# Attention with the last quarter of each head mixed by float32 matmuls, and its low halves dropped

## The reference

```python
def _L1_xattn_ref(query, key_value, Wq, bq, Wk, bk, Wv, bv, Wo, bo):
    Q = query @ Wq.T + bq          # (4, 512, 512)
    K = key_value @ Wk.T + bk      # (4, 1024, 512)
    V = key_value @ Wv.T + bv
    ...                            # into 16 heads of 32
    scores = jnp.einsum('bhsd,bhtd->bhst', Q, K) * scale
    attn = jax.nn.softmax(scores, axis=-1)
    ctx = jnp.einsum('bhst,bhtd->bhsd', attn, V)
    return ctx.transpose(0, 2, 1, 3).reshape(B, S, D_MODEL) @ Wo.T + bo
```

## Time and profile before

| | us |
|---|---|
| median of 3 runs | 1690.8 |
| lowest, highest | 1686.87, 1693.01 |
| the profiled execution, its own time | 1685.53 |
| its span, first to last instruction | 1683.8 |
| attention phase, first `maximum` to last store (window 729 to 1225) | about 496 |
| steady part, heads 0 to 56 | 405.94 |
| last seven heads | 44.93 |

### The profile page before, as it was taken

How to read it: one execution, slowest core, us unless ns; L and a number is a source line. 1 busy time by engine, 2 the same in 40 slices (tenths; PEclk the granted TensorE clock), 3 DMA queues, 4 the chain that set the end, 5 groups by cost and what they waited for, 6 DMA issues and landing times. The chain is left out here.

```text
span 1683.8 us, 27138 instructions
## 1 busy us (share of the span) xinstructions
PE 1411.4 (84%) x10011; PEld 811.6 (48%) x10087; DVE 1215.8 (72%) x1489; ACT 946.8 (56%) x1440; POOL 528.6 (31%) x403
## 2 busy tenths in 40 slices
PE   4999996999851975878998899998777699999996
PEld 3555543555430543314554555555323566666663
DVE  4888855678762878578999899999487676655551
ACT  5887833445440865406666676766622776655551
POOL 0122200000053006207887788887920000000000
PEclk7999998999965987869999999999988799999998
DMA  6788760000046439300434242533372786666640
GB/s 225 232 274 308 240 210 26 1 1 1 1 197 254 138 108 222 113 26 20 96 69 92 62 102 62 102 77 110 73 226 105 236 279 215 216 205 221 226 146 27
DMA packets 162676, 233.25 MB, mean 139 GB/s; under 512 B 46396, under 2 KB 80191, under 8 KB 161416
## 3 DMA queue, kind: packets, MB, share of 16 engines
q1 hardware_dynamic: 157064, 206.60, 40.8%
q0 software_dynamic: 5504, 25.20, 4.1%
HBM read 169.62 MB, written 55.65 MB: 134 GB/s over the span
## 5 line engine op out<-in xcount | busy, mean ns | idle before, releaser
L1707 POOL TENSOR_TENSOR t_low<-t_e 128x1024 bf16<-128x1024 f32 x192 | 375.2, 1979 | 79.2 <-DVE t_low L1796 48.7
L1750 ACT ACTIVATE t_e<-t_psE 128x512 f32<-128x512 f32 x512 | 278.0, 595 | 150.7 <-PE t_psE L1883 149.9
L1788 DVE TENSOR_REDUCE t_nmax<-t_psM 128x1 f32<-128x1024 f32 x256 | 303.4, 1215 | 27.4 <-PE t_psM L1861 26.4
L1897 PE MATMUL t_psO<-t_e,vst 128*33 128x512 bf16 x1024 | 221.4, 396 | 7.4 <-POOL t_low L1707 7.4
L1861 PE MATMUL t_psM<-kst,qst 96*64 96x512 bf16 x1024 | 176.8, 412 | 48.8 <-DVE t_nmax L1788 42.4
L2365 PE MATMUL e_psG<-late_flat,e_w1p 128*128 (+1 forms) x1536 | 171.1, 274 | 15.0 <-DVE e_hT L2309 10.3
L1883 PE MATMUL t_psE<-qst,kst 99*64 99x512 bf16 x1024 | 168.3, 387 | 1.2
L2365 PEld LDWEIGHTS e_psG<-late_flat,e_w1p 128*128 128x128 bf16 x1536 | 150.5, 98 | 35.9 <-issue 8.4
L2380 PE MATMUL e_psO<-e_w2p,e_hT 128*128 128x512 bf16 x752 | 164.9, 379 | 0.8
L1897 PE MATMUL t_psO<-t_low,vst 128*33 128x512 bf16 x512 | 155.8, 386 | 0.0
L1796 DVE TENSOR_TENSOR t_low<-t_e 128x1024 bf16<-128x1024 f32 x64 | 118.9, 1857 | 34.4 <-ACT t_e L1750 34.4
(11 more groups left out here) (262 smaller groups left out, 2300.8 us busy)
## 6 DMA issues: line engine op xcount, KB each, us to landing
piece<-in_L_ffn_w SPq DMA_DIRECT2D x32, 1024.0 KB, 13.8
xres<-in_L_ffn_w SPq DMA_DIRECT2D x32, 1024.0 KB, 14.8
wT<-ternary POOLq DMA_DIRECT2D x8, 1536.0 KB, 20.7
kst<-keys SPq DMA_DIRECT2D x96, 128.0 KB, 3.5
c_rows<-in_ctx SPq DMA_DIRECT2D x8, 1024.0 KB, 9.7
xres<-in_L_ffn_wg SPq DMA_DIRECT2D x8, 1024.0 KB, 7.0
xres<-in_L_ffn_wu SPq DMA_DIRECT2D x8, 1024.0 KB, 6.1
xres<-in_L_ffn_wd SPq DMA_DIRECT2D x8, 1024.0 KB, 6.3
```

The costliest lines, as they stand in the source:

```text
L1707: nc.gpsimd.tensor_tensor(low[:, slot(h, u), :, :], e32[:, slot(h, u), :, :], upper(h, u), ALU.subtract).then_inc(lo_pool, 1)
L1750: nc.scalar.activation(e32[:, slot(h, u), i, :], psE[:, i, :], ACT.Exp, scale=SC).then_inc(expd, 1)
L1788: nc.vector.tensor_reduce(nmax[:, h // G % 2, h % G, u:u + 1], banks_of(place_of_max(b, m)).rearrange("p a t -> p (a t)"), AX_X, ALU.max, ...
L1897: return nc.tensor.matmul(psO[side * SIDE:side * SIDE + VW, h % 2, :], values(i, r), part[:, i, :], start=first, stop=last)
```

## The change

- Quarter 3 (`FULL`) is mixed in float32: two matmuls, one for each block of 128 keys, of the float32 tile `t_e` with a new float32 values tile `t_v` (`v32`). Block 0 goes to side 0 and block 1 to side 1. No low half is made for it.
- `v32` is high plus low of `vst` (`join_values`): four joins on POOL for batch 0 before its first `max_parts`, then one join on VectorE for each group of four heads, three heads after the group's new values are asked for (`next_values`). A memset puts the ones in.
- Low halves of quarters 0 to 2 stay on POOL, and POOL no longer waits for VectorE's (`lo_dve`). In the last seven heads quarter 0 is made on VectorE.
- `t_low` shrinks from eight to six quarters. The second half of the sums lies in the keys tile instead of a tile of its own, so their load moves from head 2 to head 6 of the last batch, the sum and reciprocal on VectorE from head 5 to head 8, and the reciprocals' store from head 6 to head 9. The second spread goes into `v32`.

```diff
--- before.py
+++ after.py
...
     RING = 8
-    LO_ON_POOL = (0, 1, 2)
+    FULL = (3,)
     SIDE = P // 2
...
         e32 = sb("t_e32", [P, RING, 2, S], F32)
-        low = sb("t_low", [P, RING, 2, S], BF16)
+        low = sb("t_low", [P, RING - 2 * len(FULL), 2, S], BF16)
+        v32 = sb("t_v32", [P, G, TC, VW * G], F32)
         nmax = sb("t_nmax", [P, 2, G, 4], F32)
...
         ost = sb("t_ost", [SIDE + VW, 2, S], F32)
-        sums_more = sb("t_sums_more", [(B - 1) * NH, S], F32)
+        sums_more = kst[0:(B - 1) * NH, 0, 0, :].bitcast(F32)
         bo32 = o.pre[0:1, 1, 0, 0:3, :]
...
         bo_split = sem("t_bo_split")
-        spread = vst[:, :, :, :].rearrange("p g c n -> p (g c n)").bitcast(F32)[:, 0:PRE * KC * S].rearrange(
-            "p (b c s) -> p b c s", b=PRE, c=KC)
+        spread = [v[:, :, :, :].rearrange("p g c n -> p (g c n)")[:, 0:n].bitcast(F32).rearrange("p (c s) -> p c s", c=KC)
+                  for v, n in ((vst, 2 * KC * S), (v32, KC * S))]
         psM = c.enter_context(nc.psum_tensor("t_psM", [P, 2, 2, 512], F32))
...
         lo_dve, lo_pool = sem("t_lo_dve"), sem("t_lo_pool")
+        v32_ones, v32_ready = sem("t_v32_ones"), [sem(f"t_v32_ready{i}") for i in range(G)]
         mixed, mix_cleared, sums_added = sem("t_mixed"), sem("t_mix_cleared"), sem("t_sums_added")
...
-        def upto(quarters, head, u):
-
-            return head * len(quarters) + sum(q <= u for q in quarters)
-
-        LO_ON_DVE = tuple(u for u in range(4) if u not in LO_ON_POOL)
+        def on_pool(head, u):
+            return u not in FULL and not on_dve(head, u)
+        def on_dve(head, u):
+            return u == 0 and head >= B * NH - MAXAHEAD
+        def upto(chosen, head, u):
+            return sum(chosen(k, q) for k in range(head + 1) for q in range(4) if (k, q) <= (head, u))
         def wait_lo(eng, head, u):
-            pool = u in LO_ON_POOL
-            eng.wait_ge(lo_pool if pool else lo_dve, upto(LO_ON_POOL if pool else LO_ON_DVE, head, u))
+            if on_pool(head, u):
+                eng.wait_ge(lo_pool, upto(on_pool, head, u))
+            else:
+                eng.wait_ge(lo_dve, upto(on_dve, head, u))
...
             return (h * 4 + u) % RING
+        def low_slot(h, u):
+            return h % 2 * (4 - len(FULL)) + u
...
             return b + h // NH, h % NH, u
+        def join_values(engine, b, g):
+            halves = [vst[:, g, :, r * VW * G:r * VW * G + P] for r in range(2)]
+            return engine.tensor_tensor(v32[:, g, :, 0:P], halves[0], halves[1], ALU.add).then_inc(v32_ready[g], 1)
...
                             sp.wait_ge(stored[i], 64 * (LAST * NH // 2 + 1))
+                        sp.wait_ge(o.brows_loaded, 16)
+                    if h == 6:
+                        sp.wait_ge(mixed, (LAST * NH + G) * 4 + RING)
                         for b in range(LAST):
                             load_sums(sp, b, [v[b * NH:(b + 1) * NH, :] for v in (o.sums, sums_more)], sums_dram, o.sums_loaded)
-                        sp.wait_ge(o.brows_loaded, 16)
                     if h in (3, 4):
                         load_parts(sp, h - 3, o.pre[:, h - 3, :, :, :], mixed_dram, o.pre_loaded[h - 3])
-                    if h == 6:
+                    if h == 9:
                         sp.wait_ge(o.rsums_ready, 1)
...
                         sp.wait_ge(o.rsums_stored, 16)
-                        sp.wait_ge(mixed, ((LAST * NH) + G * (b + 2)) * 4 + RING)
-                        load_rsums(sp, b, spread[:, b, :, :], o.rsum_dram, o.rsum_loaded[b])
+                        sp.wait_ge(mixed, ((LAST * NH) + G * 2) * 4 + RING)
+                        load_rsums(sp, b, spread[b], o.rsum_dram, o.rsum_loaded[b])
...
                     head = b * NH + h
-                    if u in LO_ON_POOL:
-                        before = upto(LO_ON_DVE, head, u)
-                        if not (isinstance(before, int) and before == 0):
-                            pool.wait_ge(lo_dve, before)
+                    if on_pool(head, u):
                         pool.wait_ge(expd, head * 8 + 2 * u + 2)
-                        nc.gpsimd.tensor_tensor(low[:, slot(h, u), :, :], e32[:, slot(h, u), :, :], upper(h, u),
+                        nc.gpsimd.tensor_tensor(low[:, low_slot(h, u), :, :], e32[:, slot(h, u), :, :], upper(h, u),
                                                 ALU.subtract).then_inc(lo_pool, 1)
...
                 pool.wait_ge(zeros_set, 1)
+                nc.gpsimd.memset(v32[:, :, :, P:], 1.0).then_inc(v32_ones, 1)
+                for g in range(G):
+                    pool.wait_ge(kv_loaded[g], 16 * KV_LOADS)
+                    join_values(nc.gpsimd, 0, g)
                 max_parts(0, 0)
...
                     head = b * NH + h
-                    if u in LO_ON_DVE:
+                    if on_dve(head, u):
                         dve.wait_ge(expd, head * 8 + 2 * u + 2)
-                        nc.vector.tensor_tensor(low[:, slot(h, u), :, :], e32[:, slot(h, u), :, :], upper(h, u),
+                        nc.vector.tensor_tensor(low[:, low_slot(h, u), :, :], e32[:, slot(h, u), :, :], upper(h, u),
                                                 ALU.subtract).then_inc(lo_dve, 1)
...
                         prepare_output(b, h, u)
+                        if u == 1:
+                            next_values(b * NH + h - G - 3)
+                def next_values(head):
+                    if head >= 0 and head % G == 0 and head < LAST * NH:
+                        b, g = head // NH + 1, head % NH // G
+                        dve.wait_ge(kv_loaded[g], (b + 1) * 16 * KV_LOADS)
+                        dve.wait_ge(mixed, (head + G) * 4 + RING)
+                        join_values(nc.vector, b, g)
...
                         split_bias(h - 1)
-                    if (b, h, u) == (LAST, 5, 0):
+                    if (b, h, u) == (LAST, 8, 0):
                         dve.wait_ge(o.sums_loaded, 32 * LAST)
...
-                    p, spr = o.pre[:, b, :, :, :].rearrange("p r c s -> p r (c s)"), spread[:, b, :, :].rearrange("p c s -> p (c s)")
+                    p, spr = o.pre[:, b, :, :, :].rearrange("p r c s -> p r (c s)"), spread[b].rearrange("p c s -> p (c s)")
                     dve.wait_ge(o.pre_loaded[b], 32)
...
                     g = h // G
-                    high, rest = upper(h, u), low[:, slot(h, u), :, :]
+                    high, whole = upper(h, u), e32[:, slot(h, u), :, :]
...
+                    def add_whole(i, last):
+                        v = v32[:, g, 2 * u + i, :].rearrange("p (w h) -> p h w", h=G)[:, h % G, :]
+                        return nc.tensor.matmul(psO[i * SIDE:i * SIDE + VW, h % 2, :], v, whole[:, i, :], start=False, stop=last)
+                    if u in FULL:
+                        pe.wait_ge(expd, head * 8 + 2 * u + 2)
+                        if h % G == 0:
+                            pe.wait_ge(v32_ready[g], b + 1)
+                        add_whole(0, u == 3)
+                        add_whole(1, u == 3).then_inc(mixed, 1)
+                        return
                     if u == 0:
                         pe.wait_ge(copied_out, head + 1)
+                    rest = low[:, low_slot(h, u), :, :]
                     wait_lo(pe, head, u)
...
                 pe.wait_ge(mix_cleared, 1)
+                pe.wait_ge(v32_ones, 1)
                 for m in range(EARLY):
...
             kst = slots.enter_context(nc.sbuf_tensor("kst", [3 * HD + 3, HG, HG, T], BF16))
-            vst = slots.enter_context(nc.sbuf_tensor("vst", [P, HG, T // P, 3 * HD * HG], BF16))
+            vst = slots.enter_context(nc.sbuf_tensor("vst", [P, HG, T // P, 2 * VW * HG], BF16))
             ones_set = slots.enter_context(nc.semaphore("ones_set"))
...
```

## The result

The changed kernel takes 1643.8 us (median of 4 runs, 1641.37 to 1646.16) where the kernel before takes 1691.28 beside it: a ratio of 0.9723, 95% interval 0.9698 to 0.9748. The forecast was 1665.8. The profiled execution took 1641.37 us against 1685.53, spans 1639.6 and 1683.8, so 44.2 us are to be accounted for, not 25.

A forecast was written before the change was run, and what follows sets the result against it. VectorE was taken to bound heads 0 to 56, POOL the last seven, with TensorE bounding after the change. Savings of 17 + 6 + 2 = 25 us took 1685.5 to 1660.5, plus 5.3 for the median: 1665.8, range 1643 to 1694.

The forecast's parts named there:

- The block of 3 x 0.44 = 1.32 us: Quarter 3's mix on TensorE: four float32 records of 0.44 us, two of them overlapping, take 1.32 us instead of 0.66.
- now only the middle two can: Quarter 3's four float32 records in program order: only side 0's second and side 1's first run at once.
- x: Extra TensorE time a head for the float32 mix: 0.54 us, the middle of 0.44 and 0.66.
- The 6.12 us of an undisturbed head: TensorE's four undisturbed steps of 1.53 us each, to which the float32 extra of 0.54 is added, giving 6.66 us.
- Turnings 4 us: Heads 0 to 56: 14 turnings of a group's maxima keep 0.3 us each, 4 us on top of streaming.
- Joins, bias operations and first heads 3 + 3 us: Heads 0 to 56: VectorE's 12 joins and five bias operations cost 3 us together, filling the phase another 3.
- Sums and reciprocals 6 us: At head 56, three maxima before the end, VectorE's sums and reciprocals hold up TensorE: 6 us as before.
- Last seven heads 6 us less: POOL is the bound there; one low half goes to VectorE, so a head takes 5.6 us against 6.42: 6 us less.
- The end, 2 us: VectorE's last low half comes three steps earlier, so its quotients end with the stores: 2 us less.
- POOL's waits for VectorE's low half go too, and cost nothing: Heads 0 to 56: POOL's waits for VectorE's low half vanish at no cost, since TensorE waits for maxima, not POOL.
- records do not overlap: Rival: side 1's float32 doesn't start beside side 0's; block 1.76 us, head 7.22, 1701 us; chance 0.14.
- Float32 nearly free: Rival: a float32 record streams like bfloat16, x = 0, a head 6.12 us, 1632 us; chance 0.08.

The follow-up runs named there:

- loaded_apart: `vector_loaded` with one wait more: POOL waits before each low half until VectorE's low half of the head before is done; 1691.81 us, 1.0011 of the kernel before.
- same_side: The changed kernel with both float32 calls of quarter 3 on side 0, so they can't run beside each other; 1692.82 us, 1.004 of the kernel before.
- relief_alone: The kernel before with quarter 3's low half neither made nor used, its matmuls reading the high half, POOL not waiting for VectorE; 1634.83 us, 0.9691.
- before_no_wait: The kernel before, changed only in that POOL no longer waits for VectorE's low half of the head before; 1713.61 us, 1.0141.
- vector_loaded: The changed kernel plus VectorE's low half of quarter 3 for heads 0 to 56, into an unread tile TensorE waits on; 1713.75 us, 1.0153 of before.
- alternate: The changed kernel with float32 for quarter 3 only in even heads and the last seven; otherwise VectorE's low half, with POOL's wait; 1668.8 us, 0.9857 of before.

## Why the prediction was right, and where it was not

The direction was right, and the time lay in the range at its low edge, 22 us under the number. That 1643.8 lies inside is luck: the edge is 1643, and two of the four runs, 1641.37 and 1642.46, are below it. The gain was 47 us where 25 were forecast. Taken against its own profiled execution, the sum gave 1660.5 us and 1641.4 came; the other 2.9 us are that the median lies 2.4 above the profiled execution and not 5.3.

- **The bound passes from VectorE to TensorE: right.** VectorE waits for TensorE 176 times (it is at 81%), the clock is 1.00, and `loaded_apart` gives the old time back.
- **A float32 call is two records of twice the stream: right.** 256 records of 592 ns, 0.43 us apart on one side in `same_side`, where I had 0.44.
- **The block of 3 x 0.44 = 1.32 us: wrong, and this is the step that failed.** It measured 0.86. The step behind it was "now only the middle two can", that the sides follow the program's order. In `same_side` a call of the other side overtakes those that wait for side 0. As these rows and the 0.86 have it, each side works off its own calls in order, so side 1's float32 begins beside side 0's although it stands two records behind; over more than the four records of `same_side` no run shows it. x was to be 0.54; between `relief_alone` and the changed kernel it is 0.18, and 0.28 against the 6.12 that I counted from. 56 x 0.26 = 14.6 us of the error.
- **The 6.12 us of an undisturbed head: nearly.** `relief_alone` runs at 6.22.
- **Turnings 4 us: right.** 13 times 0.38 is 4.9.
- **Joins, bias operations and first heads 3 + 3 us: too much.** The first two heads take 0.36 us more than two others, one head 0.16; no join shows in a head's length. VectorE's joins took 1.71 us each, and its waits of 0.33 us a step or more made up for them. Each of the twelve met a low half of POOL, which took 2.87 us instead of 1.89, so that POOL's mean (780 to 1120 us) is 1.97 and not the 1.89 of the signs; no head is longer for it.
- **Sums and reciprocals 6 us: 3.8** (10.18 less 6.40). The extras together were 9.3 us, not 16. With the 14.6 above, that is the 21 us by which the first window was quicker than forecast.
- **Last seven heads 6 us less: 4.1.** A head takes 5.49, where I had 5.6. But the last is 7.48, since POOL's last two low halves took 7.87 us:

```profile
1169.97 7.87 POOL L1726 TENSOR_TENSOR t_low<-t_e 128x1024 bf16<-128x1024 f32 x2 [1.75 <-ACT t_e L1773]
```

VectorE's quotients ran at the same time:

```profile
1169.91 2.28 DVE L1872 TENSOR_TENSOR late_flat<-late_flat 128x2048 f32<-128x2048 f32 x1
1172.22 3.87 DVE L1875 TENSOR_TENSOR late_flat<-late_flat,vst 128x2048 f32<-128x2048 f32 x1
1176.02 3.98 DVE L1872 TENSOR_TENSOR late_flat<-late_flat 128x2048 f32<-128x2048 f32 x1
1180.02 2.29 DVE L1875 TENSOR_TENSOR late_flat<-late_flat,t_v 128x2048 f32<-128x2048 f32 x1
```

- **The end, 2 us: right in its mechanism, its size not shown.** The quotients end at 1182.31, 2.2 us behind the last copy instead of 6.2, and the last store is issued at 1181.75. The 1.3 us gained behind the last copy lie well within the 6.8 by which that distance differs between the traces. I had let them come earlier at no price; they came, and met POOL.
- **The start at no cost: right.** The memset took 0.19 us, the four joins 7.51 and lie in POOL's wait, of which 13.82 are left.
- **"POOL's waits for VectorE's low half go too, and cost nothing": right for this change, incomplete as a reason.** The wait kept POOL from starting a low half just ahead of VectorE's. Without it and with VectorE's low half still there, both `before_no_wait` and `vector_loaded` are 22 us slower than with it. The change is safe because the low half leaves VectorE together with the wait.

Of the rivals, "records do not overlap" is what `same_side` builds, 1692.8 us. Its head of 7.25 us is the rival's 7.22; it comes to less than the 1701 worked out because the extras beside the pace are 10.8 us there and not 16, and because its profiled execution lies 0.6 us under its median where I had added 5.3. "Float32 nearly free" (1632) was closer in time than my number but wrong as a mechanism: the record is twice as long, and it is the second side that hides half. The page FP8 and Floating Point Precision of the Trainium skill (TensorE Precision Notes), with its four passes, agrees with the traces if a pass is one stream of 0.22 us: 2 records of 0.43 us. The passes themselves no run shows. The two calls, on two sides, take their four passes at the same time.

## What to carry to other kernels

Count a narrow matmul's cost per side: add up what each side has to stream and take the larger (here 28, 29, 30 and 33 streams a head gave 6.22, 6.40, 6.57 and 7.25 us); over the few calls tried here the order in which those of the two sides stand did not matter. Before a wait between two engines is taken away as idle, ask which operations it keeps from running at once, and look for the longest instance of each of them in the trace: the median of VectorE's low halves was shorter without the wait, and the kernel 22 us slower. And work that engines do alternately balances only as far as the buffers between them let one run ahead, as `alternate` suggests; average busy shares hide that.

## What the runs showed of the hardware

- **The halves of the columns are two streams.** In `same_side` bfloat16 matmuls of side 1 start between float32 records of side 0 that the program has before them (1006.10 between 1006.09 and 1006.52), and in the changed kernel four records of 0.43 us, two on each side, take 0.86 us.
- **A float32 matmul of 33 columns of weights and 512 columns** leaves two records of 592 ns, 0.43 us apart at a clock of 1.00, with weight loads of 138 ns; the bfloat16 ones are 379 to 390, 0.22 apart, and 108.
- **VectorE and POOL hold each other up** where both work from SBUF. VectorE's low half goes from 1.2 to 2.93 us, its quotient of 2.28 to 3.98, POOL's low half from 1.89 to 5.02. They don't share: the one that starts first keeps its time, and the other is held until it is through. All 45 low halves of VectorE that start during one of POOL's in heads 0 to 56 of the kernel before, and 50 of 51 in `before_no_wait`, end 1.08 us after POOL's; alone one takes 1.22. VectorE's maxima, which read `t_psM`, ran beside POOL's low halves all the time at 1.22. The Trainium skill's GPSIMD Engine Reference, Specifications, says that POOL's access to SBUF is shared with VectorE, in contention with its instructions that have two SBUF inputs or a two-port mode; the traces agree, since low halves and quotients have two inputs and maxima have none in SBUF; no run here bears on the mode.
- **A stall costs more than its length.** In `before_no_wait` a wait of 2.59 us on TensorE, where the kernel before waits 1.02, was followed by a granted clock of 0.66 to 0.77, and the head was 3.2 us longer for a low half that took 1.57 us more.
